# Expert matmuls of layer 1 in plain fp32 instead of split fp32r halves

## The reference

```python
scores = softmax(einsum('bsd,ed->bse', hidden, gate_w)).transpose(0, 2, 1)
topk_w, topk_idx = top_k(scores, cap)            # 16 experts, cap = 512 tokens of each batch
x_tok = take_along_axis(hidden[:, None], topk_idx[..., None], axis=2)
g = einsum('becd,efd->becf', x_tok, Wg)          # 256 -> 512
u = einsum('becd,efd->becf', x_tok, Wu)
h = gelu(g) * u
eo = einsum('becf,edf->becd', h, Wd) * topk_w[..., None]   # 512 -> 256
out = scatter_add(eo) + shared                   # shared: the same net on all tokens with Ws_g, Ws_u, Ws_d
```

## Time and profile before

| | us |
|---|---|
| median of 3 runs | 4765.51 |
| lowest, highest run | 4758.56, 4766.25 |
| span of the profiled execution | 4756.4 |

### The profile page before, as it was taken

The page is one execution under the profiler, slowest core; times in us unless marked ns, Lnnn a source line. Parts: engine busy times, 40 slices in busy tenths (PEclk is TensorE's granted clock), DMA queues, the critical chain, the costliest instruction groups (busy, mean ns, idle before and its releaser), DMA issues. The chain is left out here.

```text
span 4756.4 us, 68001 instructions
## 1 busy us (share of the span) xinstructions
PE 4083.1 (86%) x24660; PEld 3380.9 (71%) x24660; DVE 3477.4 (73%) x4975; ACT 2579.2 (54%) x4869; POOL 2589.5 (54%) x1858
## 2 busy tenths in 40 slices
PE   8899999979999999978888866778888887888865
PEld 7788888858788888867777755656676666666653
DVE  5466666655566666626888889988888888888887
ACT  6544444437444444447576653256667666666655
POOL 3122222223122210026666656878999899999887
PEclk9999999989999999979999967889999999999996
DMA  2022222221122210024444431255655556556658
GB/s 90 19 97 76 85 86 76 88 87 41 52 89 73 88 58 20 22 68 141 148 143 140 141 112 60 81 173 167 192 178 179 176 186 188 173 172 190 188 164 315
DMA packets 271490, 572.90 MB, mean 120 GB/s; under 512 B 37169, under 2 KB 157746, under 8 KB 271154
## 3 DMA queue, kind: packets, MB, share of 16 engines
q1 hardware_dynamic: 246578, 534.98, 33.7%
q0 software_dynamic: 24576, 33.57, 3.9%
HBM read 445.64 MB, written 122.81 MB: 120 GB/s over the span
## 5 line engine op out<-in xcount | busy, mean ns | idle before, releaser
L1595 POOL TENSOR_TENSOR scan_drive_sb<-scan_b_wide_sb,scan_du_sb 128x1024 f32<-128x1024 f32 x512 | 1299.8, 2565 | 269.5 <-DVE scan_h_sb L1507 262.6
L1507 DVE TENSOR_TENSOR_SCAN scan_h_sb<-decay_bank,scan_state_sb,scan_drive_sb 128x512 f32<-128x512 f32 x896 | 1116.2, 1268 | 114.7 <-ACT decay_bank L1845 108.8
L1845 ACT ACTIVATE decay_bank<-scan_delta_sb,a_neg_sb 128x512 f32<-128x512 f32 x1024 | 701.0, 687 | 382.1 <-DVE scan_h_sb L1507 378.9
L1012 PE MATMUL ybank<-v_low_hi_lo_sb,pt_hi_b_sb 128*128 128x384 f32 x2048 | 665.6, 359 | 26.9 <-DVE pt_lo_b_sb L884 20.8
L1514 DVE TENSOR_TENSOR scan_ch_sb<-c_pair,scan_h_sb 128x1024 f32<-128x1024 f32 x512 | 614.2, 1200 | 63.6 <-PE c_pair L1682 63.3
L884 DVE TENSOR_TENSOR pt_lo_b_sb<-pt,pt_hi_b_sb 128x512 fp32r<-128x512 f32 x512 | 352.7, 690 | 420.1 <-ACT pt_hi_b_sb L1058 420.1
L1693 PE MATMUL y_bank<-identity_sb,scan_ch_sb 128*128 128x128 f32 x4096 | 652.2, 291 | 5.1 <-ACT scan_temp_sb L1863 5.1
L1693 PEld LDWEIGHTS y_bank<-identity_sb,scan_ch_sb 128*128 128x128 f32 x4096 | 546.2, 152 | 118.4 <-issue 19.1
L1682 PE MATMUL c_pair<-scan_cc_sb,select_state_sb 128*128 128x512 f32 x1024 | 387.1, 462 | 259.7 <-DVE scan_ch_sb L1514 259.0
L1049 ACT ACTIVATE p_b_sb<-scores,softmax_cols_b_sb 128x1024 f32<-128x1024 f32 x256 | 286.0, 1117 | 546.3 <-DVE softmax_cols_b_sb L878 409.1
L1013 PE MATMUL ybank<-v_low_hi_lo_sb,pt_lo_b_sb 128*128 128x256 f32 x2048 | 573.7, 280 | 0.0
(11 more groups left out here) (328 smaller groups left out, 9898.6 us busy)
## 6 DMA issues: line engine op xcount, KB each, us to landing
scan_b_wide_sb<-b_scratch SPq DMA_DIRECT2D x512, 512.0 KB, 3.9
w_hi_scratch<-split_hi_sb SPq DMA_DIRECT2D x51, 512.0 KB, 2.8
w_lo_scratch<-split_lo_sb SPq DMA_DIRECT2D x51, 512.0 KB, 4.1
expert_hi_sb<-w_hi_scratch SPq DMA_DIRECT2D x48, 512.0 KB, 5.4
expert_lo_sb<-w_lo_scratch SPq DMA_DIRECT2D x48, 512.0 KB, 6.4
x_b_sb<-x SPq DMA_DIRECT2D x16, 512.0 KB, 4.0
split_raw_sb<-WgT SPq DMA_DIRECT2D x16, 512.0 KB, 5.5
x_res_b_sb<-x SPq DMA_DIRECT2D x64, 128.0 KB, 4.9
```

The costliest lines, as they stand in the source:

```text
L1012: e.matmul(k.y_bank[:, 0:D + P], k.pt_hi[n % 2][:, cols], kv.v[:, block, :], start=(kb == 0), stop=False, skip_group_check=True)
L1507: e.tensor_tensor_scan(k.h[i % H_BUFFERS][:, j, :], k.decay_banks[S % DECAY_BANKS][:, :], k.drive[i % DRIVE_BUFFERS][:, j, :], start, ALU. ...
L1595: e.tensor_tensor(k.drive[i % DRIVE_BUFFERS][:, :, :], k.b_wide[i % B_BUFFERS][:, :, :], k.du[c % 2][:, :].unsqueeze(1).broadcast_to([P, P ...
L1845: e.activation(k.decay_banks[S % DECAY_BANKS][:, :], k.delta[c % 2][:, :], ACT.Exp, scale=wt.a[:, n:n + 1]).then_inc(k.s_decay, 1)
```

## The change

All matmuls of layer 1's experts (logits, gate, up, down, shared and routed) become single fp32 matmuls on the operands as they are. What belongs to the halves is gone:

- in layer 0: the loads, splits and saves of 51 weight blocks, and their landings in the fence;
- in layer 1: DVE's `xt_lo`, ACT's `h_hi`, POOL's `h_lo`, and the halves of the router's weight on POOL. ACT's copy of the transposed tokens now frees the bank. DVE's product goes to a new ring `h` of two, for which it waits until the down groups of block q - 2 are done;
- the gate copy of block q waits for the product of block q - 1 instead of for `h_lo`, and a down group waits for the products themselves;
- weights come straight from the inputs, one DMA of 512 KB for each, into a ring of six; FETCH_AT becomes (0, 4, 8), and a slot is free once the expert two before has done the same part.

```diff
 class Attention(Stage):
-        self.w_raw = self.ring("split_raw", 2, [P, 1024])
-        self.w_hi = self.ring("split_hi", 2, [P, 1024], F32R)
-        self.w_lo = self.ring("split_lo", 2, [P, 1024], F32R)
...
 def attention_sync(...):
     def residual(t):
-        if t % TILES and t <= WEIGHTS:
-            split_save(t - 1)
-        if t < WEIGHTS:
-            split_load(t)
...
-    if (b + 1) * TILES <= WEIGHTS:
-        split_save((b + 1) * TILES - 1)
...
 def attention_landings(k, b):
-            (k.s_g[1], 16 * n // 2), (k.s_xn, 16 * n)] + [
-        (sem, 32 * len(range(i, saved, 2))) for i, sem in enumerate(k.s_w_saved)]
+            (k.s_g[1], 16 * n // 2), (k.s_xn, 16 * n)]
...
 def attention_gpsimd(e, w, k, consts, b):
     def residual(t):
-        for half in range(2 if t < WEIGHTS else 0):
-            split(t, half)
...
-FETCH_AT = (0, 4, 19)
+FETCH_AT = (0, 4, 8)
+W_SLOTS = 6
...
 def moe_sync(...):
-        for half, slot in enumerate((k.w_hi[r % 4], k.w_lo[r % 4])):
-            e.dma_start(f32(slot[:, :]), w_dram[half][r]).then_inc(k.s_w[r % 4], 16)
+        e.dma_start(k.expert_w(r), raw_weight(a, r)).then_inc(k.s_w[r % W_SLOTS], 16)
...
+def wait_hidden(w, fills, q):
+    for f in (HB - 2, HB - 1):
+        fills.wait_emptied(w, "moe_up", q, f)
...
 def wait_expert_slot(w, fills, r):
+    freed_by = (wait_gate, wait_up, wait_down)[kind]
+    freed_by(w, fills, ALL_GROUPS + 2 * (expert - W_SLOTS // 3) + 1)
...
 def moe_scalar(...):
     def turn(q, c):
-        e.activation(k.xt_hi[q % 2][:, c, :], fills.bank("moe_turned", q, c), ACT.Copy).then_inc(k.s_xt_hi, 1)
+        e.activation(k.xt[q % 2][:, c, :], fills.bank("moe_turned", q, c), ACT.Copy).then_inc(fills.emptied("moe_turned", q, c), 1)
     def gate(q, f):
-        w.wait_ge(k.s_h_lo, HB * (q - 1) + f + 1)
+        if q > 0:
+            fills.wait_emptied(w, "moe_up", q - 1, f)
-    def upper(q, f):
-        e.activation(k.h_hi[:, f, :], k.g[f][:, :], ACT.Copy).then_inc(k.s_h_hi, 1)
...
 def moe_gpsimd(...):
-    def lower(q, f):
-        e.tensor_tensor(k.h_lo[:, f, :], k.g[f][:, :], f32(k.h_hi[:, f, :]), ALU.subtract).then_inc(k.s_h_lo, 1)
...
 def moe_vector(...):
-    def turn(q, c):
-        e.tensor_tensor(k.xt_lo[q % 2][:, c, :], fills.bank("moe_turned", q, c), f32(k.xt_hi[q % 2][:, c, :]),
-                        ALU.subtract).then_inc(fills.emptied("moe_turned", q, c), 1)
     def product(q, f):
-        e.tensor_tensor(k.g[f][:, :], fills.bank("moe_up", q, f), k.g[f][:, :], ALU.mult).then_inc(fills.emptied("moe_up", q, f), 1)
+        if q > 1:
+            wait_down(w, fills, q - 2)
+        e.tensor_tensor(k.h[q % 2][:, f, :], fills.bank("moe_up", q, f), k.g[f][:, :], ALU.mult).then_inc(fills.emptied("moe_up", q, f), 1)
...
 def moe_tensor(...):
     def up(q, kind, name, f):
         for c in range(DC):
-            e.matmul(bank, hi[:, c, cols], xt_hi[:, c, :], start=(c == 0), stop=False)
-            e.matmul(bank, hi[:, c, cols], xt_lo[:, c, :], start=False, stop=False)
-            last = e.matmul(bank, lo[:, c, cols], xt_hi[:, c, :], start=False, stop=(c == DC - 1))
+            last = e.matmul(bank, weight[:, c, cols], k.xt[q % 2][:, c, :], start=(c == 0), stop=(c == DC - 1))
     def down(q, j):
-        w.wait_ge(k.s_h_lo, HB * (q + 1))
+        wait_hidden(w, fills, q)
         for f in range(HB):
-            e.matmul(out, k.h_hi[:, f, rows], hi[:, f, :], start=(f == 0), stop=False)
-            e.matmul(out, k.h_hi[:, f, rows], lo[:, f, :], start=False, stop=False)
-            last = e.matmul(out, k.h_lo[:, f, rows], hi[:, f, :], start=False, stop=(f == HB - 1))
+            last = e.matmul(out, k.h[q % 2][:, f, rows], weight[:, f, :], start=(f == 0), stop=(f == HB - 1))
```

More of the change, by code:

```diff
@@ L2251, in block @@
                 gelus(q)
-        if h is not None:
-            upper(q, h)
     def shared(q, s):
@@ L2473, in block @@
     def block(q, s):
-        c, f = part(TURN_AT, s - 2), part(UP_AT, s - 1)
-        if c is not None:
-            turn(q, c)
+        f = part(UP_AT, s - 1)
         if f is not None:
@@ L2514, in logits @@
             for c in range(DC):
-                e.matmul(out, xt_hi[:, c, rows], k.gate_hi[:, c, :], start=(c == 0), stop=False)
-                e.matmul(out, xt_hi[:, c, rows], k.gate_lo[:, c, :], start=False, stop=False)
-                last = e.matmul(out, xt_lo[:, c, rows], k.gate_hi[:, c, :], start=False, stop=(c == DC - 1))
+                last = e.matmul(out, k.xt[q % 2][:, c, rows], k.gate_raw[:, c, :], start=(c == 0), stop=(c == DC - 1))
         last.then_inc(fills.filled("logits", q), 1)
@@ L2531, in up @@
         wait_turned(q)
-        hi, lo = weights(q, kind)
-        xt_hi, xt_lo = k.xt_hi[q % 2], k.xt_lo[q % 2]
+        weight = weights(q, kind)
         cols = slice(f * P, (f + 1) * P)
@@ L2831, in two_layers @@
     list_dram = scratch("list_scratch", [2, LISTS, CAPACITY])
-    w_dram = [scratch(f"w_{half}_scratch", [WEIGHTS, P, 1024]) for half in ("hi", "lo")]
     with ExitStack() as ctx:
```

102 lines of the change are left out of this document (21 added, 81 removed).

## The result

The changed kernel takes 4719.1 us (median; 4716.4 to 4720.9), the kernel before 4762.7 beside it: a ratio of 0.9914, 95% interval 0.9899 to 0.9928. That is 43.6 us less, where the prediction had 28 less; its profiled execution has a span of 4715.9 us against 4756.4. A second series gave 4718.4 us and a ratio of 0.9910 (0.9894 to 0.9927).

What follows compares the result with a forecast made beforehand. Taken as binding: TensorE's burst of gate groups, gate copy, gelus, decay, scan; DVE in the rest of a block. Layer 0's -8.4 and -11, layer 1's -13 and +4 made -28 us: 4737 us, range 4685 to 4785.

Steps and rivals of the forecast that it cites:

- Layer 0, end of the first batch: From the last softmax reciprocal to the next stage's first load, without the split and its saves: -8.4 us.
- Layer 0, tiles: 51 of 64 attention tiles lose their split, so TensorE waits less: -11 us, the other end 0.
- TensorE's pace: Layer 1 gate or up groups go from 1.47 us to 1.72 to 1.80; c_pair period in the burst 4.12 to 4.7.
- rival 4: fp32 in expert groups is slower than the convolution's pace, 0.1 us more a matmul: about 4805 us; chance 0.07.
- TensorE's cost on the path: Longer layer 1 groups add 0.9 us a block through gate copies and 0.5 through c_pair.
- DVE: Layer 1 loses two lower-part operations a block, -1.2 us, and a step of the token-turning chain, -0.3.
- ScalarE and GpSimd: In layer 1, removed upper copies on ScalarE give -0.2 us a block, removed lower subtractions on GpSimd 0.
- Rival 2: GpSimd, busiest at 91%, was the bound; a quarter of 5.9 us a block comes out: 4685 us; chance 0.15.
- The logits: Eight short matmuls fewer a block, counted only within the +4 us of layer 1's first stretch.
- Rival 1: TensorE becomes the burst's bound: +51 us, 4816; slower if over 2.0 of 3.2 us a block reach DVE; chance 0.16.
- Its milder half: Half of the burst's lag reaches the path: 66 / 2 - 15 = +18 us, 4783 us.
- Rival 3: Layer 1 loses what layer 0 gains, removed DVE time becoming waits for decay: +3 us, 4768; chance 0.18.

Runs made afterwards that it cites:

- e1: The changed kernel with layer 0's loads, splits and saves of 51 weight blocks put back; 4732.0 us.
- e4: The kernel before with all expert matmul groups as single fp32 matmuls on the upper halves, all halves still made; 4800.1 us against 4758.3.
- e8: The kernel before with only the router's logits as single fp32 matmuls on the upper halves; 4727.7 us against 4761.8.
- e5: The kernel before with only the first of three fp32r matmuls kept in gate, up and down groups; 4679.7 us, ratio 0.9825.
- e6: The changed kernel with gate and up groups spread over other steps in all blocks and the logits moved to step 17; 4716.7 us.
- e2: The changed kernel with DVE's two subtractions a block of the turned tokens put back, freeing the bank again; 4772.8 us.
- e3: The changed kernel with ScalarE's copy and GpSimd's subtraction of the product put back, four each a block, with the old waits; 4717.2 us.
- e7: The changed kernel with the product of gelu and up moved from DVE to GpSimd, ScalarE copying up out of PSUM; 4723.4 us.
- e9: The changed kernel with gate and up groups spread over other steps in routed blocks only; 4697.5 us.

## Why the prediction was right, and where it was short

**Layer 0, end of the first batch: right.** -8.4 forecast, -9.2 in the timeline (18.27 to 9.12), and e1 brought it back.

**Layer 0, tiles: right.** -11 forecast, -11.5 measured, and the waits of TensorE fell as it said they would.

**TensorE's pace: right.** 1.72 us a group and 4.7 us between broadcasts were forecast, 1.72 and 4.78 measured. The Trainium skill's sentence that the fast weight load isn't used for FP32 (TensorE: Matmul & The Clock Gate, Weight-path perf modes) had no consequence to be seen here; rival 4 is out.

**TensorE's cost on the path: right in size, wrong in its way.** The forecast's 0.9 + 0.5 us make 62 us in 44 blocks, and with 3.2 us for each of three to four blocks in the first stretch about 72. Measured is e4 less e8, both on the kernel before, so that the logits drop out: +10.6 in the first stretch, +15.3 in items 0 to 128, +37.9 in items 192 to 480, 68 in all with the small rest (76 by the runs). But of its 1.4 us a block the forecast sent 0.9 through the gate copies, the gelus and the decay, and 0.5 through c_pair. Between e8 and e4 DVE's wait for decay in items 192 to 480 doesn't grow (78.9 to 75.4), while that for c_pair grows from 36.7 to 68.4: nearly all of the cost came through c_pair. With the short groups of e5 it was still 72.9. So the length of TensorE's groups did not set the wait behind the gelus, as the prediction's chain of burst, gate copy, gelus, decay and scan had it; their place did matter (60.4 in e6). That the two parts add up to the right cost is luck.

**DVE: a little large.** 1.2 + 0.3 us a block were forecast, 66 us; e2 measured 51 by the stretches, 54 by the runs. In items 192 to 480, the same work in both kernels, DVE's busy time is 34 us lower (1193.1 to 1158.9, forecast about 40 for 32 blocks), and its waits for decay and c_pair together are 23 us higher (121.7 to 144.7, forecast about the same 40).

**ScalarE and GpSimd: 0.2 forecast, none measured.** e3, which puts the work back, has +3 by the stretches and -1 by the runs, against 9. Rival 2 is out: the engine with the highest occupancy was not the one that mattered, and the Trainium skill's rule to improve that one first (Perfetto Trace Analysis, Identifying the Most-Contended Engine) would have misled here; GpSimd at 91% and at 81% gave the same time.

**The logits: the step that failed.** The forecast counted "eight short logits matmuls" less as a part of the +4 in the first stretch and as nothing beside the scan, which is worth about -3 us in all (eight times 0.11 us in three to four blocks). Measured is -25 in the stretches with logits, -28 in all of layer 1 and -34 by the runs of e8; put back as 24 fp32 instructions, +19 to +24 in the same stretches and +16 by the runs. Two things were overlooked, both in the trace of before. The group stands on TensorE just ahead of an up group whose product DVE waits for, so what it takes is on the path in a shared block. And it did not take 2.6 us each time: with some groups at half clock it took 50.1 us in 16 blocks, 3.1 each. Forecasting the first stretch and the shared blocks at the routed blocks' rates left that out. The forecast's -28 against -41 in the profile is this one term with smaller ones of both signs. It also decided layer 1: of the 25 to 29 us that layer 1 gained about nothing is left without it, where the forecast had 9. The whole would have become faster by layer 0's 18 us alone; that layer 1 went the forecast's way is luck.

**The sum and what stays open.** Layer 1's terms as measured one at a time, -28 (logits), +68 (the other groups), -51 (DVE), -3 (ScalarE and GpSimd), make -14 us; layer 1 got 25 to 29 us shorter. The runs give much the same: -34, +76, -54, +1. Some 11 to 15 us belong to what was not tried by itself (half the weight traffic, the ring of six slots, the relaxed waits) or to the terms' working on each other. With 8 us between two executions of one kernel in the longest stretch that can't be divided further. Rival 1 (TensorE as the bound of the burst) is true in a sense that the sign doesn't show: DVE waits 24 us more for c_pair. Its milder half in the prediction, +18 us, is a slip: half of the lag is 1.6 us a block against 1.7 saved, which by its own sentence on where the sign turns is no loss at all. Rival 3's way is out, as DVE's wait for decay didn't grow; its result, that layer 1 gains nothing, is about what is left without the logits, but by TensorE's 68 us.

## What to carry to other kernels

Price each stretch with its own rows, and ask of every group on an in-order engine what stands right behind it: eight tiny matmuls fewer in a 2.6 us group were worth more than all that was taken off ScalarE and GpSimd, because a group that others waited for came next. Putting a saving back (e2) gives its price with little else changed; moving work on to other engines (e7) can make a wait of its own there, so look at the waits of every engine before reading such a run as "this time was worth nothing". A sum that comes out right can have its parts on the wrong path: check each part's wait. Where a step table sets the order, moving groups by a few steps (e9, 11 to 15 us of layer 1) can be worth half as much as changing what they compute (25 to 29 us), and it should be tried separately for stages that hold different work.

## What the runs showed of the hardware

A matmul of 128 x 16 took 0.11 us as fp32r and as each of the two instructions of an fp32 one, 0.21 us at the lower level of the clock, so for such short ones fp32 makes fewer instructions (16 instead of 24) at the same price each. With 512 columns the price was 0.43 us for each of two against 0.23 for each of three fp32r ones: 0.86 against 0.69 to 0.74 us. In items 192 to 480 the granted clock was 0.86 in e5, where TensorE was busy for 931 us, and 0.97 in the changed kernel, where it was busy for 1227. Less work did not always go with a lower clock: in items 0 to 64 TensorE was busy for 275 of 308 us at 0.92 in the kernel before and for 261 of 297 us at 0.95 in e8. What the clock cost or gave back in time, no run separates.
